# A graph network's three edge-sum layers: a chunk of four tiles first, a full chunk last, and the last chunk's node block ahead of its sums

## The reference, cut to what matters

```python
h = relu(layernorm(x))
x = x + attention(h, edges)              # softmax over the edges of each node, weighted sum of messages
h = relu(layernorm(x))
for l in range(3):                       # sage_conv, three times
    msg  = relu(h @ pW[l] + pb[l])[src]
    agg  = segment_sum(msg, dst)         # the sum over the edges of each node
    mean = agg / max(degree, 1)
    out  = mean @ lW[l] + lb[l] + h @ rW[l]
    h    = out / norm(out)               # silu after the first two layers
return x + layernorm(h) * ln_w + ln_b
```

## Time and profile before

| | |
|---|---|
| Time, median of three | 4324.89 us |
| Profiled execution | 4331.38 us, span 4328.1 us |
| Clock granted to PE, mean | 0.806 |
| PE busy | 3184.3 us (74%) |
| POOL busy | 2614.6 us (60%) |
| DVE busy | 1551.3 us (36%) |
| ACT busy | 1019.3 us (24%) |
| First gather of layers 0, 1, 2 | 1736.6, 2603.8, 3460.9 us |
| Last gather's end, layers 0, 1, 2 | 2568.8, 3424.5, 4277.6 us |

### The profile page before, as it was taken

The page is one execution under the profiler, slowest core; times in us unless marked ns, Lnnn a source line. Parts: engine busy times, 40 slices in busy tenths (PEclk is TensorE's granted clock), DMA queues, the critical chain, the costliest instruction groups (busy, mean ns, idle before and its releaser), DMA issues. The chain is left out here.

```text
span 4328.1 us, 43372 instructions
## 1 busy us (share of the span) xinstructions
PE 3184.3 (74%) x12616; PEld 1839.6 (43%) x12616; DVE 1551.3 (36%) x5417; ACT 1019.3 (24%) x2512; POOL 2614.6 (60%) x2736
## 2 busy tenths in 40 slices
PE   7388888767777764488797865888888657778774
PEld 4266666544555552243343332433333333333332
DVE  5166765534444433021222230222222403333434
ACT  4255555433433332011111120111111200000000
POOL 1466566666666663666665646666666466666663
PEclk9588788867777666698898987889988878888886
DMA  6488888544444441566565625666665267666652
GB/s 187 142 262 261 253 262 265 161 126 132 137 131 132 130 113 31 167 216 195 177 200 174 192 81 165 213 185 195 198 189 180 79 182 222 193 200 207 202 179 71
DMA packets 477460, 755.99 MB, mean 175 GB/s; under 512 B 120022, under 2 KB 313832, under 8 KB 477221
## 3 DMA queue, kind: packets, MB, share of 16 engines
q1 hardware_dynamic: 349940, 411.84, 29.2%
q0 software_dynamic: 126896, 341.33, 28.1%
q10 hardware_dynamic: 384, 0.00, 0.0%
HBM read 651.42 MB, written 101.44 MB: 174 GB/s over the span
## 5 line engine op out<-in xcount | busy, mean ns | idle before, releaser
L1158 POOL DMA_INDIRECT ring<-message_table,src_index x1689 | 1609.7, 953 | 999.7 <-issue 473.9
L1224 PE MATMUL ps<-ring,attention_work 128*128 128x512 f32 (+1 forms) x2352 | 1080.7, 599 | 171.6 <-issue 107.9
L559 POOL DMA_INDIRECT ring<-attention_table,src_index x784 | 757.1, 966 | 506.2 <-issue 210.0
L1224 PEld LDWEIGHTS ps<-ring,attention_work 128*128 128x128 f32 x2352 | 480.6, 212 | 622.4 <-issue 565.6
L1717 PE MATMUL ps<-ring,one_hot 128*128 128x265 f32 x1568 | 626.4, 512 | 148.1 <-issue 146.8
L1294 PE MATMUL ps<-ring,attention_work 128*32 128x256 f32 x3378 | 367.9, 428 | 177.1 <-issue 172.2
L1717 PEld LDWEIGHTS ps<-ring,one_hot 128*128 128x128 f32 x1568 | 349.6, 246 | 244.0 <-issue 212.0
L1449 ACT ACTIVATE ring<-ps 128x256 f32<-128x256 f32 (+1 forms) x213 | 81.5, 383 | 1375.2 <-DMA attention_work<-run_flags 1220.5
L1678 PEld LDWEIGHTS ps<-attention_work 128*128 128x128 f32 x1568 | 317.5, 246 | 100.3 <-issue 29.1
L1364 DVE TENSOR_TENSOR attention_work<-attention_work,ps 128x160 f32<-128x160 f32 (+2 forms) x246 | 69.4, 294 | 802.0 <-DMA root<-in_x 620.1
L1382 DVE SCALAR_TENSOR_TENSOR block_o<-ps,inv_deg,root 128x256 f32<-128x256 f32 x147 | 71.1, 483 | 682.4 <-remote 397.2
(11 more groups left out here) (167 smaller groups left out, 3122.3 us busy)
## 6 DMA issues: line engine op xcount, KB each, us to landing
ring<-dense_adjacency SPq DMA_DIRECT2D x441, 256.0 KB
attention_work<-message_table SPq DMA_DIRECT2D x588, 128.0 KB
attention_work<-in_dst_edges SPq DMA_DIRECT2D x112, 448.0 KB
dense_adjacency<-root SPq DMA_DIRECT2D x49, 896.0 KB
ring<-message_table,src_index POOLq DMA_INDIRECT x1689
ring<-dense_adjacency SPq DMA_DIRECT2D x147, 128.0 KB
attention_sums<-sums_out SPq DMA_DIRECT2D x112, 132.5 KB
ring<-attention_table,src_index POOLq DMA_INDIRECT x784
```

Source lines behind the costliest of these rows:

```text
L559: pool.indirect_dma_start(m.ring[:, k, t, 0:cols], None, table, bass.IndirectOffsetOnAxis(ap=m.src[:, at:at + 1], axis=0)).then_inc(s[f"ro ...
L1158: pool.indirect_dma_start(m.quad_ring[:, k, j, :], None, m.tables[w.l], bass.IndirectOffsetOnAxis(ap=m.src[:, t:t + 1], axis=0)).then_inc( ...
L1224: last = nc.tensor.matmul(m.ps[:, 2 + half, 0:cols], m.m_rows[:, k, half * P:(half + 1) * P], m.a_rows[:, k, 0:cols], start=(j == 0), stop ...
```

## The change

Three things change.

1. The first chunk of a layer has four tiles (`BEGUN`), all others have eight, the last one too. There are still 71 chunks. `FIRST_TILE` becomes 218, so a layer has 564 tiles, and `OWN` becomes 230. `chunk_tiles`, `window_base` and the new `window_cols` say which tiles and node columns a chunk has. The slots of the node blocks and `steps_done` stay as they were.
2. In the last chunk PE does `flip(69)` and the node block's work (`turn`, `combine`, `project`) ahead of both quads' sums.
3. In the last chunk ACT does `keep(70)` behind the node block's work.

In `prepare`, the list of places is made with two iotas on POOL for one, and with six additions on DVE for four.

```diff
-FIRST_TILE = (DENSE - MARGIN) // PITCH
-WORK = -(-(LAST_TILE - FIRST_TILE) // WIDTH)
+BEGUN = WIDTH // 2
+WORK = -(-(LAST_TILE - (DENSE - MARGIN) // PITCH - BEGUN) // WIDTH) + 1
+FIRST_TILE = LAST_TILE - (WORK - 1) * WIDTH - BEGUN
+BEGUN_PAIRS = BEGUN // DEPTH
...
+def chunk_tiles(q):
+    at = FIRST_TILE + q * WIDTH - (WIDTH - BEGUN if q else 0)
+    return range(at, at + (WIDTH if q else BEGUN))
+
+def window_base(q):
+    return PITCH * chunk_tiles(q)[0] - MARGIN
+
+def window_cols(q):
+    return PITCH * len(chunk_tiles(q)) + 2 * MARGIN
...
 # PE, chunk(q)
+                    def node():
+                        if i is not None:
+                            turn(w, i - 1)
+                            dense((done + steps_done(q) + 1) // 2)
+                            combine(w, i, q)
+                        dense(steps_done(q))
+                        if i is not None:
+                            project(w, i - 1)
+
+                    if q == WORK - 1:
+                        flip(w, q - 1)
+                        node()
                     pe.wait_ge(s["onehot"].sem, s["onehot"].done(u))
                     pe.wait_ge(s["kept"].sem, s["kept"].free(u))
                     sums(0)
-                    if q:
+                    if 0 < q < WORK - 1:
                         flip(w, q - 1)
                     sums(1)
-                    if i is not None:
-                        turn(w, i - 1)
-                        dense((done + steps_done(q) + 1) // 2)
-                        combine(w, i, q)
-                    dense(steps_done(q))
-                    if i is not None:
-                        project(w, i - 1)
+                    if q < WORK - 1:
+                        node()
...
 # ACT, chunk(q)
-                    keep(w, q)
+                    if q < WORK - 1:
+                        keep(w, q)
                     if i is not None:
                         first(w, i)
                         second(w, i)
+                    if q == WORK - 1:
+                        keep(w, q)
...
 # DVE, merge(q)
-                fresh = min(VIEW, BLOCKS * P - base) - again
+                fresh = min(window_cols(q), BLOCKS * P - base) - again
```

More of the change, by code:

```diff
@@ L204, in _ @@
             nc.gpsimd.memset(m.node_rows.rearrange("p k j c -> p (k j c)"), 0.0).then_inc(s["blank"].sem, 1)
-            nc.gpsimd.iota(m.lane_at[:], [[-WIDTH * PITCH, WORK]], base=MARGIN - PITCH * FIRST_TILE, channel_multiplier=1,
+            nc.gpsimd.iota(m.lane_at[:, 0:1], [[0, 1]], base=-window_base(0), channel_multiplier=1,
+                           allow_small_or_imprecise_dtypes=True)
+            nc.gpsimd.iota(m.lane_at[:, 1:WORK], [[-WIDTH * PITCH, WORK - 1]], base=-window_base(1), channel_multiplier=1,
                            allow_small_or_imprecise_dtypes=True)
@@ L408, in windows @@
                     for j in range(LANES):
-                        chunks = (PAIRS - j + LANES - 1) // LANES
                         rows = slice(j * LANE, (j + 1) * LANE)
-                        nc.vector.scalar_tensor_tensor(m.lane_at[rows, 0:chunks], m.pair_first[rows, j::LANES], float(-j * LANE),
-                                                       m.lane_at[rows, 0:chunks], ALU.add, ALU.add)
+                        for some, pairs in ((m.lane_at[rows, 0:1], slice(j, min(j + 1, BEGUN_PAIRS))),
+                                            (m.lane_at[rows, 1:WORK], slice(BEGUN_PAIRS + j, PAIRS, LANES))):
+                            if pairs.start < pairs.stop:
+                                nc.vector.scalar_tensor_tensor(some, m.pair_first[rows, pairs], float(-j * LANE), some, ALU.add, ALU.add)
             def run_facts(piece):
@@ L1029, in node_slots @@
 def node_slots():
-    base = PITCH * FIRST_TILE - MARGIN
-    taken = {-(-((n + 1) * P - base) // (WIDTH * PITCH)): n for n in range(DENSE_BLOCKS, BLOCKS - 1)}
+    taken = {min(q for q in range(WORK) if window_base(q) >= (n + 1) * P): n for n in range(DENSE_BLOCKS, BLOCKS - 1)}
     for part in range(PASSES):
@@ L1080, in walk @@
             second(i)
-def chunk_tiles(q):
-    at = FIRST_TILE + q * WIDTH
-    return range(at, min(at + WIDTH, LAST_TILE))
 def quad_tiles(v):
@@ L1103, in landed @@
     return 16 * sum(len(quad_tiles(x)) for x in range(v % QUADS, v + 1, QUADS))
-def window_base(q):
-    return PITCH * FIRST_TILE - MARGIN + q * WIDTH * PITCH
 def ring_pieces(at, cols):
@@ L1331, in compare @@
                 dve.wait_ge(s["summed"].sem, s["summed"].free(u))
-                at = q * WIDTH
+                at = tiles[0] - FIRST_TILE
                 nc.vector.tensor_tensor(m.lane_hot[:, u % 2, 0:len(tiles), :], m.iota_row[:, None, 0:LANE].to_broadcast([P, len(tiles), LANE]),
```

## The result

| | before | after |
|---|---|---|
| Median | 4326.61 us (4320.71 to 4331.87, 4 runs) | 70788.65 us (70774.90 to 70793.68, 4 runs) |
| Profiled execution | 4331.38 us | 70774.90 us, span 70773.0 us |
| Clock granted to PE, mean | 0.806 | 0.504 |

The ratio is 16.339, with a 95% interval of 16.309 to 16.368. The forecast was 4323.6 us and its range 4311 to 4338. No term of that sum, and no rival, is within a factor of sixteen of this, so the question is not where a layer loses time but what the program ran at all.

The account below looks back on a forecast made before the run. A layer was taken to go at POOL's gather pace, then by the chain of node blocks; -16.5 + 10.4 + 3.0 + 0.45 + 1.3 = -1.3 us gave 4323.6 us from a median of 4324.89, range 4311 to 4338.

Parts of the forecast that it names:

- the attention phase: One more indirect transfer L568 between gathers in a phase at POOL's pace: +1.3 us, bounds 0 and 1.3.
- Start of a layer: 44 gathers before POOL's first stop instead of 48, stop 7.8 us instead of 8.3: -5.5 us a layer, -16.5 in three.
- Rival A: POOL's first stop in a layer shrinks to an ordinary one, about 2 us: 4305.9 us in all; chance 0.08.
- rival B: POOL's first stop grows to 13.3 us, so the layer's start gives nothing: 4340.1 us in all; chance 0.10.
- End of a layer: Five more gathers for chunk 70 delay chunk 66: +5.4, +4.5 and +0.5 us in the three layers, sum +10.4.
- Order in the last chunk: keep(70) queues behind h of block 47, delaying combine(48): +1.5 us each in layers 0 and 1, +0.45 in layer 2.
- The middle "unchanged within 5 us": A layer's middle, 64 chunks of eight gathers before and after, costed at nothing and expected unchanged within 5 us.
- the sign of a wrong base: If a layer's middle moves by more than 5 us, the pace hangs on where stops fall, not on counts.
- a short stop: In a layer's middle, each chunk costs ten us of gathers and a POOL stop of 1.90 us until an older chunk is summed.
- the terms of 16 and 14 us: The layers' start, -16.5 us, against losses chiefly at their end, +10.4, and in the last chunk's order, +3.0 and +0.45.
- Gathers beside DVE: Gathers average 0.953 us with DVE at work beside most, so rows show no lockout price; the rule would add a few tenths.
- Rival C: Last gathers still land when the node block starts, hiding its 6.7 us behind them: -16.4, 4307.2 us; chance 0.04.

Follow-up runs that it names:

- e1: The changed kernel with the padding edges at node 6270 instead of 6271: 3626.83 us, 0.9971 of the kernel before.
- e2: The kernel before with the irregular-edge count's limit on distance inside a pair at 23 instead of 32: 70640.89 us (1 run).
- e7: The changed kernel, padding still at node 6271, with the count's limit on distance inside a pair at 33 instead of 32: 4289.18 us (1 run).
- e3: The changed kernel with LAST_TILE one higher, so the first tile is odd (219), padding and limit as they were: 4292.32 us, ratio to before 1.0011.
- e0: The kernel before with only the padding moved to node 6270, on a slower chip: 4298.12 us, ratio to before 1.0019.
- e8: e1's kernel run again in the third group, against the kernel before: 3629.07 us, ratio 0.9971.
- e10: The kernel before with only the padding moved to node 6270, on a faster chip: 3641.32 us (1 run).

## Why the prediction was wrong, step by step

**The step that failed** is in how the sum was set up: "So I price four stretches: the start of a layer, its end, the order in the last chunk, and the attention phase." There is a fifth place ahead of them, the branch behind `prepare`, and it has no term, no rival and no share of the range. `FIRST_TILE` = 218 came into the sum only as one more L568 and one more gather per layer, and the changes to `prepare` as "a few tenths beside loads: 0". They were priced as instructions; what they compute was not followed to who reads it. What ran in place of the priced path was the five passes of `any_tile`, 70.8 ms of one tile at a time. e1, e2 and e7 each change one constant that decides this branch, e3 the parity of the first tile; the time follows by 66 to 67 ms each way. A chance of 0.11 for slower over a range that ends at 4338 had no room for it.

**Given the planned path, on the slower kind of chip**, for which the sum was made, its steps can be read off e7 and e3, one execution each. POOL in e7, the first 44 gathers and the stop of layer 0, the stop of layer 1, the tail of layer 0:

```profile
1703.00:1758.00 55.00, 41.88 (x44) 0.62 0.59 179
1758.00:1765.20 7.20, 0.00 (x0) 0.50 0.21 61
2617.40:2624.90 7.50, 0.04 (x1) 0.50 0.20 57
2527.20:2562.70 35.50, 0.02 (x1) 0.92 0.09 31
```

- *Start of a layer.* 44 gathers in 55.0 us: as forecast (55.1). The stop, 7.8 forecast, was 7.2, 7.5 and 7.5 us where before had 8.2, 8.3 and 8.1, and e3 had 7.2 to 7.4. Rival A (2 us) and rival B (13 us) are out. From a layer's first gather to the end of the stop it is 62.2 us in e7 and was 68.1: 5.9 us less, 5.5 forecast.
- *End of a layer.* The forecast had chunk 66's copy 11.6 us behind chunk 65's. It came 9.5 us behind it in e7 and 14.3 in e3 (10.1 and 13.6 in layer 1), where before had 6.2 and e0, the old code on the same chip, 8.2. So the period of a chunk isn't a constant that eight gathers bring with them. ACT in e7, keep(65), keep(66), h of block 47, keep(70), h of block 48, and then keep(65) and keep(66) in e3:

```profile
2517.28 0.38 ACT L1465 ACTIVATE ring<-ps 128x256 f32<-128x256 f32 x1 [5.30 <-DMA attention_work<-run_flags]
...
2526.77 0.38 ACT L1465 ACTIVATE ring<-ps 128x256 f32<-128x256 f32 x1 [5.57 <-DMA attention_work<-run_flags]
...
2548.66 0.51 ACT L1489 ACTIVATE block_h<-block_o,block_inv_norm 128x256 f32<-128x256 f32 x1 [2.01 <-DVE block_inv_norm L766]
2549.07 0.36 ACT L1465 ACTIVATE ring<-ps 128x256 f32<-128x256 f32 x1
...
2555.01 0.51 ACT L1489 ACTIVATE block_h<-block_o,block_inv_norm 128x256 f32<-128x256 f32 x1 [2.00 <-DVE block_inv_norm L766]
```

```profile
2517.40 0.38 ACT L1465 ACTIVATE ring<-ps 128x256 f32<-128x256 f32 x1 [4.83 <-DMA attention_work<-run_flags]
...
2531.70 0.38 ACT L1465 ACTIVATE ring<-ps 128x256 f32<-128x256 f32 x1 [7.20 <-DMA attention_work<-run_flags]
```

- *Order in the last chunk.* keep(70) stands directly behind the h of block 47, as forecast, and PE in e7 has combine(48) 2.15 us behind that h (2548.66 to 2550.81), forecast 2.3, before 0.84. The sums of chunk 70 hide behind the node block:

```profile
2543.02 0.76 PE L1245 MATMUL ps<-attention_work,ring 128*128 128x144 f32 x4 [0.50 <-DVE attention_work L1358]
...
2544.46 1.13 PE L1271 MATMUL ps<-w_l,attention_work 128*128 128x256 f32 x4 [0.46 <-DVE attention_work L1380]
...
2547.23 1.07 PE L1303 MATMUL ps<-ring,attention_work 128*32 128x256 f32 x16
2549.49 0.76 PE L1245 MATMUL ps<-attention_work,ring 128*128 128x144 f32 x4 [1.19 <-ACT ring L1465]
...
2550.81 1.13 PE L1271 MATMUL ps<-w_l,attention_work 128*128 128x256 f32 x4 [0.35 <-DVE attention_work L1380]
```

- *Whole layers.* The table has each layer from its first gather to the next layer's first (layer 2 to the end of the span), and the tails, from a layer's last gather's end on, all in us. The forecast's terms give the changes in its row, and tails of 35.6, 36.1 and 45.1 us.

| | first gather | layer 0 | layer 1 | layer 2 | tails |
|---|---|---|---|---|---|
| before | 1736.6 | 867.2 | 857.1 | 867.2 | 35.0, 36.4, 50.4 |
| e0, old code | 1724.9 | 857.9 | 857.8 | 858.9 | 37.0, 36.9, 50.2 |
| e3, the change | 1710.7 | 858.1 | 857.7 | 862.1 | 39.9, 40.6, 52.5 |
| e7, the change | 1703.0 | 859.7 | 865.5 | 856.7 | 35.5, 34.9, 45.4 |
| forecast of the change | | +1.4 | +0.5 | -4.6 | |

e7's tails fit the forecast and e3's don't, being 4 to 7 us longer. Against e0 the three layers are 3.3 us longer in e3 and 7.3 in e7, where the terms said 2.7 shorter: what the start gives is taken back later in the layer. The old code itself differs by 17 us between its two executions (on two chips), and the time ahead of the layers differs by up to 34 us among the four, where the sum had only +1.3. So single executions settle the start and the order in the last chunk, but not the sizes of the end or of a whole layer.
- *The middle "unchanged within 5 us"* can't be read from one execution either. From the first stop's end to a layer's last gather, before took 764.1 and 752.6 us in layers 0 and 1 and e0 752.8 and 753.0, with 515 gathers. With 520, for which the forecast adds 6.3 us, e3 took 755.9 and 754.9 and e7 762.0 and 768.4. That the pace hangs on where the stops fall, which the prediction named as the sign of a wrong base, is what the rows suggest: "a short stop" behind each chunk isn't there, but 48 stops of 1.0 to 8.2 us in layer 0 of before, and e7 has one of 11.3 us in layer 1.
- *The sum.* Forecast -1.3 us of some 4300, that is a ratio of 0.9997; e3 has 1.0011 with an interval from 0.9992 to 1.0029. That nothing would be measurable was right for a path that the changed kernel does not take. That the terms of 16 and 14 us cancel so closely is not shown: the interval alone is 16 us wide, and the term for the end of a layer missed.
- *Gathers beside DVE.* The prediction says that DVE is at work beside most gathers and that the rows show no price. In layer 0 of before DVE is at work beside 225 of the 515 gathers behind the first stop, and there is a small price: gathers with nothing beside them last 0.947 us and at most 0.96, the 62 beside the one-hot comparison (L1333) 0.984 and up to 1.18. For a layer that is some 2 us of POOL. The old code shows it in e0 and e10 as well (0.979 and 0.977 us).

**Rival C**, 0.04, holds on the faster kind of chip: the node block hides behind the gathers. It was excluded by "the last gather ends at 2568.8 and flip(69) comes 17.7 us later", which holds where the sums lag behind POOL (e7: from 2527.2 to 2543.0, 15.8 us) and not where they don't (e1: flip(69) at 2145.43, ahead of the last gather's end). Its price of 16.4 us fits e1's tails, -16.9, by chance as much as by reason, since it was made for two layers and e1 gained 6.1, 4.7 and 6.1 us in three.

**The version that beats both.** The change with the padding at 6270 (e1, e8) takes 0.9971 of the kernel before on the faster kind of chip, twice. On the slower kind nothing was shown faster (e3 1.0011, with an interval that holds 1), and the version with the padding at 6270 was not run there. It is also one node from the same fall: its farthest distance is 31, one below the limit, so another edge list can trip the count.

## What to carry to other kernels

A kernel that chooses its path at run time has its largest price in the choice: look in the trace for a value that every engine loads, find the branch behind it, and evaluate its condition on the inputs for every constant that the change moves (here the parity of a first tile, against padding at the last node). When a result is off by a factor, compare instruction counts and the lines that are missing before any duration. And when a small difference of large terms is forecast, the chip whose pace the terms were read from decides it: the same change showed no gain where the sums lag behind the gathers (e3) and 0.3% where they don't (e1, e8).

## What was not expected of the hardware

The same code differs by 18% between chips (4290.94 and 3637.25 us), and PE's granted clock differs by less (0.81 and 0.88). On the slower kind, while POOL issues gathers back to back, the other engines often start again together when POOL pauses. In e0, DVE, ACT and POOL, the last behind a stop of 3.29 us:

```profile
2001.90 0.32 DVE L1364 TENSOR_TENSOR attention_work<-attention_work,ps 128x160 f32<-128x160 f32 x1 [10.79 <-DMA root<-in_x]
2002.00 0.38 ACT L1449 ACTIVATE ring<-ps 128x256 f32<-128x256 f32 x1 [10.67 <-DMA attention_work<-run_flags]
2002.23 0.94 POOL L1158 DMA_INDIRECT ring<-message_table,src_index  x1 [3.29 <-DMA attention_work<-run_flags]
```

The copies come 11.6 us apart during gathers and 5 to 6 us apart as soon as they end, and the gathers stop 8 us at a layer's start. PE's busy time is higher too, 3132.3 us in e0 against 2868.6 in e10, for the same x12616. The mean DMA rate is lower (176 against 208 GB/s), but that only says that the same 755.99 MB took longer. On the faster kind POOL gathers 563 tiles of a layer without a stop. The other path, where a tile never has more than a few transfers in flight, takes nearly the same time on both (70788.65 us, and 70640.89 in one run). What in the chip makes the difference was not tried, and that the pauses of POOL let the results out, rather than the results ending the pauses, is not shown.
